# In the last stage, the sum of the experts' two result arrays moves from VectorE to GpSimd

## What is computed

```python
    mixed_output = jnp.sum(topk_expert_outputs * topk_weights[..., None], axis=2)
    ...
    s = _L1_attn_ref(xn, L1_attn_ab, L1_attn_h_0)
    g = _silu(_L1_ffn_ref(xn, ...))        # the mixture above
    x = x + s * g
    return x
```

## Time and profile before

| | |
|---|---|
| median of 3 runs | 1512.23 us (1511.62 to 1512.91) |
| the profiled execution's own time | 1508.08 us |
| its span | 1506.3 us |
| last stage, first load issued to the span's end | 1467.8 to 1506.3 us |
| DVE busy over the span | 997.9 us (66%) |
| POOL busy over the span | 554.0 us (37%) |

### The profile page before, as it was taken

One profiled execution on the slowest core, in us unless ns is written; L12 is line 12 of the kernel. 1 busy time (PEld: TensorE's weight loads), 2 busy tenths in 40 slices (PEclk: granted clock), 3 DMA queues, 4 the chain that ended last, 5 costly groups with the idle time before them and its releaser, 6 DMA issues. The chain is left out here.

```text
span 1506.3 us, 29415 instructions
## 1 busy us (share of the span) xinstructions
PE 1309.6 (87%) x8092; PEld 669.3 (44%) x8092; DVE 997.9 (66%) x2343; ACT 868.9 (58%) x1661; POOL 554.0 (37%) x543
## 2 busy tenths in 40 slices
PE   5899999999999999999989998657884599999970
PEld 2433433434343343343433334234432488888770
DVE  1878888888888888888867885234443254444448
ACT  0277787788778778778867875212221244444332
POOL 2122342342343234224224215355555244444440
PEclk9999999999999999999989998779996799999995
DMA  6333222312312322231231232368773223222229
GB/s 222 105 97 111 91 73 73 107 55 70 107 55 74 110 92 72 71 108 55 70 108 52 75 94 68 94 219 282 254 245 99 77 71 90 78 65 66 62 58 334
DMA packets 116391, 162.27 MB, mean 108 GB/s; under 512 B 17874, under 2 KB 52370, under 8 KB 116051
## 3 DMA queue, kind: packets, MB, share of 16 engines
q1 hardware_dynamic: 103842, 137.73, 28.2%
q0 software_dynamic: 8448, 17.58, 3.4%
q10 hardware_dynamic: 4016, 6.05, 1.3%
HBM read 104.20 MB, written 49.77 MB: 102 GB/s over the span
## 5 line engine op out<-in xcount | busy, mean ns | idle before, releaser
L775 DVE TENSOR_REDUCE row_max<-ps_max 128x2 f32<-128x1024 f32 x512 | 614.9, 1219 | 137.2 <-PE ps_max L1032 133.5
L983 ACT ACTIVATE probs<-ps_exp 128x512 f32<-128x512 f32 x1024 | 556.3, 597 | 132.1 <-PE ps_exp L1032 114.1
L1032 PE MATMUL ps_exp<-q_op,k_op 32*128 32x512 f32 x1024 | 352.3, 502 | 26.9 <-ACT probs L983 19.9
L1032 PEld LDWEIGHTS ps_exp<-q_op,k_op 32*128 32x128 f32 x1024 | 145.9, 184 | 410.1 <-ACT probs L983 368.8
L1113 PE MATMUL ps_y<-probs,v_aug 128*32 128x512 f32 x2048 | 279.0, 617 | 0.2 <-ACT y_raw L989 0.2
L1032 PE MATMUL ps_max<-k_op,q_op 32*128 32x512 f32 x1024 | 255.4, 498 | 2.6 <-DMA k_op<-k_parts_scratch 1.6
L1579 ACT ACTIVATE hidden<-ps_h,b 128x256 f32<-128x256 f32 x268 | 118.7, 474 | 157.4 <-PE ps_h L1553 147.0
L1622 POOL DMA_INDIRECT y_scratch<-result,goes_to x134 | 128.4, 958 | 154.7 <-DVE result L1607 128.6
L671 POOL TENSOR_TENSOR rstd<-var_eps,minus_half 128x4 f32<-128x4 f32 x32 | 32.8, 1026 | 366.5 <-DVE var_eps L770 366.5
L315 POOL DMA_INDIRECT sorted_scratch<-rows,place x120 | 116.1, 967 | 88.8 <-issue 31.7
L1560 PE MATMUL ps_o<-w,hidden 128*128 128x128 f32 x1072 | 131.3, 276 | 0.0
(11 more groups left out here) (185 smaller groups left out, 1483.8 us busy)
## 6 DMA issues: line engine op xcount, KB each, us to landing
q_op<-q_parts_scratch SPq DMA_DIRECT2D x16, 1024.0 KB, 5.7
k_op<-k_parts_scratch SPq DMA_DIRECT2D x16, 1024.0 KB, 8.4
q_op<-k_pad_scratch SPq DMA_DIRECT2D x15, 1024.0 KB
k_op<-k_pad_scratch SPq DMA_DIRECT2D x15, 1024.0 KB
unit_rows<-sorted_scratch SPq DMA_DIRECT2D x136, 66.0 KB
q_parts_scratch<-qk_split SPq DMA_DIRECT2D x16, 512.0 KB, 3.1
k_parts_scratch<-qk_split SPq DMA_DIRECT2D x16, 512.0 KB, 2.9
q_parts_scratch<-qk_split SPq DMA_DIRECT2D x16, 256.0 KB, 2.4
```

Of the source, the lines that this page charges most:

```text
L775: dve.tensor_reduce(row_max[group // 2][:, t, head:head + 2], ps_max[u][:, :, :], AX.X, ALU.max)\
L983: act.activation(probs[s % 2][:, i, :], ps_exp[i % 2][:, :], ACT.Exp).then_inc(exp_done, 1)
L1032: return pe.matmul(out, lhsT, rhs, start=True, stop=True)
```

## The change

`mix` leaves DVE's program. POOL gets a program in this stage, which it did not have: for each batch in order it waits for both loads and adds, and signals `mixed_ready` as DVE did. DVE's loop is now gate_s(b), finish(b). Loads, stores, ACT's program, sizes and buffers stay.

```diff
         @block.vector
         def _(dve):
-            def mix(b):
-                dve.wait_ge(y_loaded[b], 32)
-                dve.tensor_tensor(y_first[:, b, :], y_first[:, b, :], y_second[b], ALU.add).then_inc(mixed_ready, 1)
-
             def gate_s(b):
...
-            mix(0)
             for b in range(B):
-                if b + 1 < B:
-                    mix(b + 1)
                 gate_s(b)
                 finish(b)
+
+        @block.gpsimd
+        def _(pool):
+            for b in range(B):
+                pool.wait_ge(y_loaded[b], 32)
+                pool.tensor_tensor(y_first[:, b, :], y_first[:, b, :], y_second[b], ALU.add).then_inc(mixed_ready, 1)
```

## The result

| | before | after the change |
|---|---|---|
| median of 22 runs each | 1511.41 us | 1519.3 us |
| lowest to highest | 1505.35 to 1518.03 | 1513.58 to 1527.37 |
| the profiled execution's span | 1506.3 us | 1525.3 us |
| last stage, first load issued to the span's end | 38.5 us | 44.7 us |
| first addition started to last finish ended | 32.40 us | 38.63 us |

The ratio is 1.0048 with a 95% interval of 1.0036 to 1.0061: slower by 5.4 to 9.2 us of 1511.41. The two profiled executions differ by 19 us, but 12.8 of these were there when the last stage began: its first load was issued at 1467.80 before and at 1480.57 after, behind code that the change does not touch.

A forecast was written before the change was run, and what follows sets the result against it. DVE's chain of waits bounds the kernel, with full DMA queues close behind. Fifteen turns of 1.70 us, then 10.6 us of DVE alone, end DVE 6.4 us later: 1512.23 + 6.4 = 1518.6 us, 8 in 10 from 1514.5 to 1524.

The forecast's parts named there:

- The turns: Last stage: POOL's additions and DVE's instructions alternate, each waiting for the other, 0.54 + 1.16 = 1.70 us a pair.
- The phases: Last stage: 15 pairs in turn take 25.5 us, then DVE's other 16 instructions run alone for 10.6 us.
- The end: Behind DVE's end: no store backlog, the last store still needs 2.75 us, and DVE ends 6.4 us later.
- Whole records in turn: Last stage: nothing of either engine's start-up is hidden, 2.03 us a pair, 5 us more: 1523.6 us; chance 0.15.
- DVE keeping the ports: Last stage: POOL gets in only when DVE waits for a SiLU, 5.09 us per two batches: 1522.1 us; chance 0.13.
- Real overlap with the DMA as the limit: Last stage: long instructions share the ports, DMA limits, gain of 2 us at most: 1510.2 us; chance 0.10.
- The floor: Last stage: the least time the full DMA queues allow, leaving a gain of 2 us at most.

The follow-up runs named there:

- halves: The changed kernel with each POOL addition issued as two of 128x256; first addition to last finish 37.93 us, stage 44.0 us, ratio to the kernel before 1.0057.
- gate_psum: The changed kernel with only the mix_gate buffers in PSUM; first addition to last finish 29.17 us, stage 37.1 us, ratio to the kernel before 0.9995.
- both_psum: The changed kernel with the mix_gate buffers and gate_s's product in PSUM; first addition to last finish 24.95 us, stage 37.2 us, ratio to the kernel before 0.9978.

## Why the prediction was right

**The turns.** Predicted: DVE and POOL alternate one to one, 1.70 us a pair. Measured: alternation throughout, 1.67 us. The hand-overs can be read in the middle: DVE ends at 1501.92 and 1503.59, and the addition between (started 1501.33, some 1.71 long) at 1503.04. That is 1.12 us after DVE (predicted 1.16) and DVE 0.55 after POOL (predicted 0.54). Both came from single rows of layer 0, of other shapes.

**The phases.** From the first addition's start: the last stretched DVE instruction ends at 28.0 us (predicted 28.15), then 16 DVE instructions run alone for 10.6 us (predicted 10.6), in all 38.63 (predicted 38.75). Two small errors cancelled in part. Load 1 landed 3.07 us after load 0 instead of 2.04, so POOL began its second addition late. The first turns were cheaper than 1.70, as DVE was still waiting for a SiLU: POOL's timeline has the second to fourth additions (4.31 us from 1487.02) at 1.44 us each, where a turn later took 1.67.

**The end.** The last store's 2.75 us stayed (1522.58 to 1525.3), and no stores piled up. The stage grew by 6.2 us; forecast 6.4. The runs say 5.4 to 9.2, with 7.9 us between the medians; they can't tell 6.4 from 7.9. That the forecast of 1518.6 us lies only 0.7 below the measured 1519.3 is in part luck: it was counted from 1512.23, the median of three runs, which is 0.8 above the median of 22.

**The rivals.** Whole records in turn: no, the start-up of each side stayed hidden. DVE keeping the ports: no, a waiting POOL gets in every time; halves shows it for shorter instructions as well. The argument against this rival was too narrow, though. It counted on DVE's wait for itself between gate_s and finish, but POOL gets in just as well between finish and the next gate_s, where DVE waits for nothing: the SiLU for the gate_s that starts at 1501.84 had ended at 1497.6, and still an addition of POOL went first, which ended at 1503.04, 1.12 us after the end of the finish ahead of it. The row that spoke for the rival, L842 starting ahead of L671, is a DVE instruction with one tensor input. gate_s in gate_psum, with one input in SBUF, never waited for POOL either, which fits; a tensor_scalar like L842 was not tried. Real overlap with the DMA as the limit: not in this kernel, but both_psum made that case. I had put its stage at 36.5 us; it took 37.2. The floor was right in kind and 0.7 us low.

**What stays open.** By up to 19 us executions differ before the last stage starts (first load issued between 1467.8 and 1487.2 in nine profiles), which was not followed up. It hides 1 to 2 us in any of the ratios, so the small gain of both_psum and gate_psum is shown for the stage alone.

## What to carry to other kernels

Before moving elementwise work from VectorE to an idle GpSimd, look at where VectorE's inputs lie during that stretch: with two in SBUF it stood still here for most of each GpSimd addition that read SBUF, 0.95 to 1.07 us for one of 1.27 that saved it 0.60. One input in PSUM made the overlap real; then ask whether anything is behind it, which here was a full DMA queue and left a stage 1.3 us shorter than before the change, though DVE ended 7.5 us earlier in it. A few rows, in which a small instruction of one engine ended just behind a longer one of the other, were enough to see it and to put a price on it beforehand.

## What the runs showed of the hardware that was not expected

The waiting for the ports lies inside the records of both engines, so DVE's busy time in the page rose (997.9 to 1001.6 us over the span, 30.5 to 34.3 in the last stage) though it executed 16 instructions fewer, and the table of waits names none of it. The other unexpected thing is how regular the turns are: over 16 additions, the changed kernel shows no case of two from one engine while the other was waiting.
